# Head compaction and its row sums moved from ScalarE to VectorE in a windowed-attention and feed-forward kernel

## The reference

```python
disp = (x @ W_disp)  # 16 heads x 16;  val = (x @ W_val)  # 16 heads x 64
strain = disp_win - disp[:, :, :, None, :]          # 64 neighbours of every token
bond_act = gelu(strain @ W_strain + rel_emb @ W_pos)
bond_logits = (bond_act @ W_bond)[..., 0]
damage_act = gelu(strain @ W_dmg + b_dmg)
damage = sigmoid((damage_act @ W_dmg_out)[..., 0] + b_dmg_out[0])
logits = where(cmask, bond_logits - 10.0 * damage, -inf)
weights = softmax(logits)                           # over the 64 neighbours
out = einsum('bntd,bntde->bnte', weights, val_win)
x = x + out @ W_cproj
# then: x = x + sigmoid(xr @ W_r) * (relu(xk @ W_k)**2 @ W_v), of layernorm(x)
```

## Time and profile before

| | us |
|---|---|
| median of 2 runs (3258.12 to 3258.42) | 3258.27 |
| the profiled execution | 3263.7 |
| span of its slowest core (core 3) | 3262.1 |
| spans of the 8 cores | 3247.4 to 3262.1 |

### The profile page before, as it was taken

One profiled execution on the slowest core, in us unless ns is written; L12 is line 12 of the kernel. 1 busy time (PEld: TensorE's weight loads), 2 busy tenths in 40 slices (PEclk: granted clock), 3 DMA queues, 4 the chain that ended last, 5 costly groups with the idle time before them and its releaser, 6 DMA issues.

```text
span 3262.1 us, 21899 instructions; the slowest of 8 cores (3247.4 to 3262.1 us)
## 1 busy us (share of the span) xinstructions
PE 1702.0 (52%) x4568; PEld 469.6 (14%) x4568; DVE 757.2 (23%) x1930; ACT 1210.0 (37%) x2044; POOL 17.3 (1%) x32
## 2 busy tenths in 40 slices
PE   0065455435554445425555535455555556777776
PEld 0011111101111111101111112112211111111111
DVE  0012223233221333322212211111122242232101
ACT  0014556565555655754434443333211111111010
POOL 0000000000000000000000000000000000000000
PEclk9998665556565556656555555555555555555555
DMA  8300000010000100030100011101121101101001
GB/s 132 102 23 10 14 6 19 4 20 10 20 10 4 20 10 10 4 61 29 33 26 26 26 30 36 36 26 33 49 61 55 39 13 39 39 20 39 26 26 45
DMA packets 134679, 100.44 MB, mean 31 GB/s; under 512 B 111120, under 2 KB 112288, under 8 KB 134560
## 3 DMA queue, kind: packets, MB, share of 16 engines
q1 hardware_dynamic: 125152, 78.88, 8.9%
q0 software_dynamic: 9408, 20.15, 3.2%
HBM read 74.86 MB, written 35.40 MB: 34 GB/s over the span
## 4 chain that ended last, share of the span: by engine, by line
PE 42%; ACT 27%; issue 19%; DVE 6%; DMA 5%; ACTq 1%; DVEq 0%; SPq 0%
ACT s_actT L443 11%; ACT s_actT L433 6%; PE ps L697 5%; PE ps L929 5%; PE ps L901 5%; PE ps L875 5%; PE ps L283 5%; DMA Ebuf<-s_zero 4%; PE ps L456 4%; ACT s_eh L498 3%; PE ps L621 2%; PE ps L617 2%; PE ps L304 2%; PE ps L646 2%; PE ps L640 2%
## 5 line engine op out<-in xcount | busy, mean ns | idle before, releaser
L456 PE MATMUL ps<-s_actT,s_bd 128*32 128x512 bf16 (+1 forms) x1280 | 465.7, 512 | 634.6 <-ACT s_actT L443 460.1
L443 ACT ACTIVATE s_actT<-s_argT,s_pcols 128x512 bf16<-128x512 bf16 (+1 forms) x640 | 368.3, 646 | 43.2 <-DVE s_argT L422 31.0
L422 DVE TENSOR_TENSOR s_argT<-s_dD 128x512 bf16<-128x512 bf16 (+1 forms) x640 | 203.6, 380 | 395.3 <-ACT s_actT L433 232.8
L433 ACT ACTIVATE s_actT<-s_argT,s_bdmgc 128x2048 bf16<-128x2048 bf16 x128 | 256.2, 2002 | 62.0 <-DVE s_argT L422 50.5
L456 PEld LDWEIGHTS ps<-s_actT,s_bd 128*32 128x32 bf16 x1280 | 126.4, 120 | 947.9 <-issue 935.8
L422 DVE TENSOR_TENSOR s_argT<-s_dS 128x512 bf16<-128x512 bf16 (+1 forms) x640 | 203.6, 380 | 222.8 <-ACT s_actT L443 158.5
L697 PE MATMUL ps<-s_wcp,s_atok 128*128 128x512 bf16 x272 | 155.6, 572 | 49.5 <-ACT s_atok L670 10.0
L929 PE MATMUL ps<-s_wval,s_kact 128*128 128x512 bf16 x256 | 149.5, 584 | 60.2 <-DVE s_x2r L938 23.8
L875 PE MATMUL ps<-s_xk,s_wkT 128*128 128x512 bf16 x256 | 149.5, 584 | 58.4 <-DVE s_xk L861 20.3
L283 PE MATMUL ps<-s_wval,s_lnfm 128*128 128x512 bf16 x272 | 145.3, 534 | 49.3 <-ACT s_lnfm L272 9.6
L901 PE MATMUL ps<-s_wrT,s_xr 128*128 128x512 bf16 x256 | 149.5, 584 | 38.2
(11 more groups left out here) (110 smaller groups left out, 1279.4 us busy)
## 6 DMA issues: line engine op xcount, KB each, us to landing
s_wbt<-Ebuf SPq DMA_DIRECT2D x68, 191.0 KB, 3.3
Ebuf<-s_zero SPq DMA_DIRECT2D x16, 544.0 KB
X2buf<-s_xrel SPq DMA_DIRECT2D x17, 512.0 KB, 2.6
s_x<-X2buf POOLq DMA_DIRECT2D x17, 512.0 KB, 3.9
s_xt<-xs SPq DMA_DIRECT2D x33, 256.0 KB, 4.2
s_xrel<-xs SPq DMA_DIRECT2D x33, 256.0 KB, 4.2
s_x2r<-X2buf SPq DMA_DIRECT2D x16, 512.0 KB, 3.7
out<-s_x2r SPq DMA_DIRECT2D x16, 512.0 KB, 2.7
```

What stands on the lines that cost most here:

```text
L422: (lambda e: e.tensor_sub(s_arg[slot][:, 0:W], srcT[:, srcOff + c0 - 63 + j: srcOff + c0 - 63 + j + W], srcT[:, srcOff + c0: srcOff + c0 + ...
L433: P.emit("scalar", (lambda half=half: (lambda e: e.activation(out=s_actT[:, 2048 * half:2048 * half + 2048], in_=s_argT[:, 2048 * half:204 ...
L443: P.emit("scalar", (lambda slot=slot, W=W, bias=bias: (lambda e: e.activation(out=s_act[slot][:, 0:W], in_=s_arg[slot][:, 0:W], func=AF.Ge ...
L456: (lambda e: e.matmul(PS[bank][32 * q:32 * q + 32, 0:W], s_bd32[:, pi * 128 + v * 32: pi * 128 + v * 32 + 32], s_act[slot][:, 0:W], start= ...
```

## The change

The 16 compactions per block go from ScalarE (`activation`, Copy, with an accumulator output) to VectorE (`tensor_scalar`, times 1.0, with an accumulator output that adds). All 17 blocks are affected, 272 instructions. The waits follow: the copy to `s_etok` no longer waits for ScalarE, the reciprocal no longer waits for it either, and the dumps of a chunk wait for VectorE's count. What the first head of a chunk waits for is the same, but it is VectorE that waits.

```diff
             P.emit("vector", ... e.tensor_copy(s_etok[ts % 2][:, :], PSB[bank][:, 0:1024]) ...
-                waits={"st": P.now("st"), "ss": css.get(ts - 1, 0)}, inc="sv")
+                waits={"st": P.now("st")}, inc="sv")
...
-                P.emit("scalar", (lambda srcap=srcap, hG=hG, ts=ts, zc=zc: (lambda e: e.activation(
-                    out=s_eh[:, hG * 256 + ts * 64: hG * 256 + ts * 64 + 64], in_=srcap,
-                    func=AF.Copy, accum_out=s_zsum[:, zc:zc + 1])))(),
-                    waits=wvv if hG == 0 else None, inc="ss")
-            css[ts] = P.now("ss")
+                P.emit("vector", (lambda srcap=srcap, hG=hG, ts=ts, zc=zc: (lambda e: e.tensor_scalar(
+                    out=s_eh[:, hG * 256 + ts * 64: hG * 256 + ts * 64 + 64], in0=srcap,
+                    scalar1=1.0, scalar2=None, op0=ALU.mult, op1=ALU.add,
+                    accum_out=s_zsum[:, zc:zc + 1])))(),
+                    waits=wvv if hG == 0 else None, inc="sv")
+            css[ts] = P.now("sv")
             P.emit("vector", ... e.reciprocal(s_zrec ..., s_zsum ...) ...
-                waits={"ss": css[ts]}, inc="sv")
+                inc="sv")
             compact_ts[ts] = P.now("sv")
         compact_done[ci] = P.now("sv")
-        cd_ss = P.now("ss")
+        cd_ss = P.now("sv")
...
             P.emit("sync", ... e.dma_start(out=dstp, in_=srcp) ...
-                   waits={"ss": cd_ss, "dz": dz_all} if hG == 0 else None,
+                   waits={"sv": cd_ss, "dz": dz_all} if hG == 0 else None,
                    inc=DE_SEMS[hG % 4], amt=16)
```

## The result

The changed kernel takes 3227.0 us (median), the kernel before 3258.9 us. The ratio is 0.9899, 95% interval 0.9887 to 0.9911: 31.9 us or 1.0% faster, where 3230 us (28 us) was forecast. By the 2% bound that is no change; against the interval it is a clear one.

The account below looks back on a forecast made before the run. The compaction on ScalarE was taken to set the time in its stretches, 4.9% of the span. 24.2 us from 16 blocks plus 4.0 us in chunk 4 made 28.2 us, off the median 3258.3: 3230 us, range 3206 to 3258.

Parts of the forecast that it names:

- 2% bound: Whole kernel: 65 us, about what a measurement can tell from no change; "same" got a chance of 0.95.
- The path: Compaction stretches, 158 us or 4.9% of the span: one engine works at a time, so savings reach the next chunk.
- Rival C: Compaction isn't on the path and only chunk 4 gains: 3254 us; chance 0.04, together with the clock alone.
- The blocks: 16 blocks of chunks 0 to 3: each falls from 9.23 to 7.72 us, 1.51 us less, 24.2 us together.
- The head: One compaction instruction with its accumulator read on VectorE: 0.33 + 0.08 = 0.41 us start to start, against 0.50 on ScalarE.
- Rival B: The accumulator's read on VectorE costs nothing visible: 0.30 us a head, 56 us faster, 3202 us; chance 0.10.
- Rival A: The accumulator's read is serial on VectorE: 0.59 us a head, 17.9 us slower, 3276 us; chance 0.12.
- Chunk 4: Evacuation L624 no longer stands behind the compaction in ScalarE's queue, so TensorE runs on earlier: 4.0 us gained.
- The dumps' wait: VectorE's first head of a chunk waits for the previous chunk's dumps, issued long before: costs nothing.
- The dumps' later issue: Dump DMAs L513 wait for the last reciprocal, 0.25 + 0.11 us later, 5 times: taken as nothing, 1.8 us at most.
- ScalarE's busy time: Profile after: ScalarE's busy time down by some 136 us to about 1074, VectorE's up by 75 to 85.
- The gap: Between VectorE instructions that wait for the one before on their own engine: 0.106 us, counted in every head.

## Why the prediction was right

- **The path.** That the compaction is bare, and that each microsecond per block goes through, held: 16 blocks and chunk 4 give 30.7 us of the 31.9, and the stretches between are unmoved. Rival C (3254 us), other work behind which the compaction hides, is out. The dies' mean granted clock stayed within the hundredth that was set as a bound (0.586 to 0.585 and 0.584 to 0.588).
- **The blocks.** 24.2 us was forecast for the 16 blocks, 26.6 measured. A block without a pause came out at 7.50 us and not 7.72, mostly because a head takes 0.398 us and not 0.41; 16 x (9.23 - 7.50) would be 27.7 us. The pauses, those for the dumps among them, are larger in sum after than before and took back about 1 us. The prediction had read a block without a pause and counted none in either kernel.
- **The head.** 0.41 us was forecast, 0.398 measured. Its parts came out otherwise. The prediction had 0.22 us for the main instruction, 0.11 us of gap and 0.08 us added by the read. The trace has 0.265 us for the main one (0.045 more, by the stride), a read that begins 0.075 us before its end and adds only 0.01 us (its busy time is 0.083 us, near the memset's 0.06 and not the 0.15 I had counted), and 0.125 us of pause. The sum is right partly because two errors cancel, and that part was luck: the read's price was a choice between two neighbours, not a row.
- **Two instructions.** The Trainium skill ("VectorE: DVE Perf Modes", Two Vector instructions with no wait between them) says that an accumulator output makes a second instruction; the trace agrees, 272 DVE_READ_ACCUMULATOR rows. Rival B, no visible read at 0.30 us a head (3202 us), is out. Its price is near that of the kernel without the accumulator output, 0.32 us a head.
- **Rival A**, a read that runs wholly behind, didn't come: 0.083 us, not 0.26.
- **Chunk 4.** 4.0 us forecast, 4.1 in the trace, 4.2 by itself on the chip. It was the surest term, since it rested on no unknown price.
- **The dumps' wait** was put at nothing and costs about 0.3 us on the path in each of chunks 1 to 3, although long fulfilled: about 1 us.
- **The dumps' later issue** was put at nothing, with up to 1.8 us in the range. It starts 0.33 us behind the start of chunk 0's last reciprocal, where before it started 0.09 us ahead of it, and nobody shows it: 356.6 us to the next compaction before, 356.4 after.
- **ScalarE's busy time** was to fall by 136 us. It fell by 110, from 1210.0 to 1099.6. The two L498 groups overlap by 0.09 us per head, so their busy times can't be added. VectorE's rose by 74 us (forecast 75 to 85).
- **The gap** of 0.106 us, which stood in the sum as a constant, was the largest matter left, and I didn't ask what it would be worth. The kernel's runner puts a wait between any two heads although no head reads what another writes. The runs without it gave 50 us on VectorE and 54 us on ScalarE, both more than the change itself. So the forecast was right about this change, but the move to another engine was the smaller part of what these heads had to give.

## What to carry to other kernels

Where many small instructions of one engine stand in a row, read the start-to-start time, not the row's duration, and ask which part of it is a wait of the engine for itself. Independent instructions need no wait between them: leaving it out was worth 0.21 us of 0.40 on VectorE and 0.20 of 0.50 on ScalarE, more than the move from one engine to the other (0.10). Better still here was to take them together in a few instructions with larger access patterns (3.3 us a block against 4.3 without the waits). A queue that holds up somebody else's evacuation is a term of its own; here it could be read from the trace to a tenth of a microsecond.

## What the runs showed of the hardware

- Two VectorE instructions without a wait between them overlap: 0.185 us start to start for a main instruction of 0.26 us and a read of 0.085 us. The Trainium skill ("VectorE: DVE Perf Modes", The DRAIN you can't avoid) says that the drain of the pipe can't be skipped by chaining instructions without semaphores, and adds that a next one which isn't held starts earlier. Here leaving out the wait took a head from 0.40 to 0.185 us, so for these short ones the measurement decides against the first and agrees with the second.
- On VectorE it is the wait that costs and not the count: 3176.8 us with every head counting, 3177.0 us with one.
- On ScalarE the accumulator's read is a row of 0.19 us. Without the waits the next head starts 0.09 us after the read does, 0.30 us start to start in place of 0.50.
- tensor_scalar with an accumulator output on 64 bf16 elements takes 0.265 us in steps of 8 elements, and 0.22 us dense (with max in place of the multiplication); without the accumulator output it takes 0.216 us in steps of 8.
- Four waits on semaphores long reached held VectorE's next instruction back by about 0.3 us (1.09 to 0.81 us from copy to head).
